# Self-attention scores of a one-layer graph network: the squares' off-diagonal block computed once and turned with the cross products, in one score buffer of two banks

## The reference

```
u     = x @ x.T / sqrt(384)                      # 256 x 256 scores, symmetric
p     = softmax(u);  delta = p * adj
attn  = delta / (sum(delta, axis=2) + 1e-10)
h_w   = x @ W_w.T + b_w                          # w in left, self, right
ctx   = (attn, j>i) @ h_left + diag(attn) * h_self + (attn, j<i) @ h_right
x     = layernorm(x + relu(layernorm(ctx) * gamma + beta))
```

## Time and profile before

| | |
|---|---|
| three runs | 472.43, 472.1, 472.37 us; median 472.37 |
| the profiled execution | 471.55 us, of which the span of the trace is 469.8 |
| TensorE busy | 456.4 us, 97% of the span |
| VectorE busy | 357.2 us, 76% |
| ScalarE busy | 325.3 us, 69% |
| GpSimd busy | 222.7 us, 47% |
| granted TensorE clock, mean | 0.996 of full speed |

### The profile page before, as it was taken

How to read it: one execution, slowest core, us unless ns; L and a number is a source line. 1 busy time by engine, 2 the same in 40 slices (tenths; PEclk the granted TensorE clock), 3 DMA queues, 4 the chain that set the end, 5 groups by cost and what they waited for, 6 DMA issues and landing times.

```text
span 469.8 us, 9613 instructions
## 1 busy us (share of the span) xinstructions
PE 456.4 (97%) x2714; PEld 452.4 (96%) x2714; DVE 357.2 (76%) x1087; ACT 325.3 (69%) x714; POOL 222.7 (47%) x294
## 2 busy tenths in 40 slices
PE   8999899999999999999999999999999999999992
PEld 6999899999999999999999999999999999999981
DVE  5777877777788777888777887777778877787766
ACT  7663787676687677677667678767668767767752
POOL 0115556544445543445554445654444554444552
PEclk9999999999999999999999999999999999999998
DMA  8476455566365566445566545555545556644211
GB/s 260 144 226 201 136 185 184 193 192 192 112 205 186 179 191 201 153 160 185 172 204 197 162 160 174 185 190 190 186 141 176 185 182 190 203 142 136 82 67 67
DMA packets 84582, 80.72 MB, mean 172 GB/s; under 512 B 7122, under 2 KB 76756, under 8 KB 84564
## 3 DMA queue, kind: packets, MB, share of 16 engines
q1 hardware_dynamic: 84560, 80.51, 53.6%
q10 hardware_dynamic: 4, 0.00, 0.0%
HBM read 51.91 MB, written 28.57 MB: 171 GB/s over the span
## 4 chain that ended last, share of the span: by engine, by line
PE 90%; POOL 3%; DVE 3%; issue 1%; ACT 1%; POOLq 0%; DVEq 0%
PE ps_proj L449 59%; PE ps_ctx L484 20%; PE ps_scores L441 4%; PE ps_scores L432 4%; PE ps_scores L395 1%; POOL shifted L1017 1%; POOL scaled L1013 1%; POOL rstd L1007 1%; PE ps_ctx L402 1%; DVE stats L774 1%; ACT normed L593 0%; PE ps_proj L490 0%; DVE xt_lo L706 0%; POOL dt_left L1001 0%; POOL dt_right L1001 0%
## 5 line engine op out<-in xcount | busy, mean ns | idle before, releaser
L449 PE MATMUL ps_proj<-w_hi,xt_hi 128*128 128x384 f32 x576 | 193.9, 337 | 2.1 <-ACT ps_proj L563 2.1
L449 PE MATMUL ps_proj<-w_lo,xt_hi 128*128 128x384 f32 x576 | 193.7, 336 | 0.0
L449 PE MATMUL ps_proj<-w_hi,xt_lo 128*128 128x384 f32 x576 | 193.6, 336 | 0.0
L1007 POOL TENSOR_TENSOR rstd<-var_eps,minus_half 128x4 f32<-128x4 f32 x32 | 43.8, 1368 | 182.7 <-DVE var_eps L793 180.2
L449 PEld LDWEIGHTS ps_proj<-w_hi,xt_hi 128*128 128x128 f32 x576 | 108.5, 188 | 2.7 <-ACT ps_proj L563 2.7
L449 PEld LDWEIGHTS ps_proj<-w_lo,xt_hi 128*128 128x128 f32 x576 | 108.3, 188 | 0.0
L449 PEld LDWEIGHTS ps_proj<-w_hi,xt_lo 128*128 128x128 f32 x576 | 108.2, 188 | 0.0
L567 ACT ACTIVATE proj_hi<-ps_proj 128x384 fp32r<-128x384 f32 x128 | 63.4, 496 | 55.5 <-PE ps_proj L449 55.0
L563 ACT ACTIVATE ps_proj<-bias 128x384 f32<-128x384 f32 (+1 forms) x192 | 92.9, 496 | 4.2 <-DVE proj_lo L759 3.9
L1013 POOL TENSOR_TENSOR scaled<-normed,gamma_sb 128x384 f32<-128x384 f32 x62 | 63.1, 1018 | 36.6 <-ACT normed L593 30.5
L759 DVE TENSOR_TENSOR proj_lo<-ps_proj,proj_hi 128x384 fp32r<-128x384 f32 x128 | 68.1, 547 | 13.5 <-ACT proj_hi L567 13.5
(11 more groups left out here) (86 smaller groups left out, 663.6 us busy)
## 6 DMA issues: line engine op xcount, KB each, us to landing
x_sb<-in_x SPq DMA_DIRECT2D x32, 384.0 KB, 4.4
xt_sb<-in_x_t SPq DMA_DIRECT2D x31, 384.0 KB, 3.8
out_dram<-out_sb SPq DMA_DIRECT2D x31, 384.0 KB, 2.9
adj_sb<-in_adj SPq DMA_DIRECT2D x32, 256.0 KB, 4.5
dt_dram<-turned SPq DMA_DIRECT2D x31, 256.0 KB, 2.0
dt_raw<-dt_dram SPq DMA_DIRECT2D x124, 64.0 KB, 2.0
cross_dram<-cross_turned SPq DMA_DIRECT2D x30, 256.0 KB, 2.1
cross_raw<-cross_dram SPq DMA_DIRECT2D x120, 64.0 KB, 2.0
```

The lines of the kernel that those rows point to most:

```text
L449: mm = nc.tensor.matmul(ps_proj[bank(at, g)][:, 0:H], stationary, moving[w][:, c, :], start=False, stop=True, skip_group_check=True)
L1007: nc.gpsimd.tensor_tensor(rstd[at.slot(2)][:], var_eps[:], minus_half[:], ALU.pow).then_inc(rstd_ready, 1)
```

## The change

The high and low parts of `x_t` now stand side by side in one tile, `xt_split`, so that one matmul can take keys of both. `squares` is gone. `cross(ahead)` does nine matmuls: for the first row tile, hi by hi of all 256 keys and hi by lo of all 256 keys; for the second row tile one matmul for each chunk with 384 columns (hi by hi of its own tile, hi by lo of both tiles). A row of `ps_scores` now has three blocks of 32 columns in each of the four groups (squares of the own tile, and two for what becomes the scores), in a bank of its own for each row tile. There is one such buffer instead of two. `turn_cross` transposes the last two blocks, so the squares' off-diagonal block, computed only in the first row tile, reaches the second one by the transpose.

`finish_scores` no longer waits for TensorE in these batches, but first adds the squares of the own tile onto `cross_raw` (a new instruction, with the semaphore `own_added`). `cross(ahead)` waits for the deltas of `ahead - 1`, which is `nxt`; before it was `ahead - 2`. Three batches instead of two are done in full; the third, batch 2, stands in batch 1 behind the first projection. On ScalarE `seed_proj(at, 4)` stands ahead of `exps(nxt)` in all batches; before it was so in batch 1 alone.

```diff
-    IN_FULL = 2
+    IN_FULL = 3
...
-        xt_hi = [sb(f"xt_hi{i}", [P, C, L], F32R) for i in range(UNROLL)]
-        xt_lo = [sb(f"xt_lo{i}", [P, C, L], F32R) for i in range(UNROLL)]
+        xt_split = [sb(f"xt_split{i}", [P, C, 2 * L], F32R) for i in range(UNROLL)]
...
-        ps_scores = [psum(f"ps_scores{i}", [P, T, L]) for i in range(2)]
+        ps_scores = psum("ps_scores", [P, T, BANK])
...
+        def blocks(t):
+            return ps_scores[:, t, 0:3 * P].rearrange("p (q k c) -> p q k c", q=Q, k=3)
+
+        def exponentials(t):
+            return ps_scores[:, t, 0:3 * P].rearrange("p (q e) -> p q e", q=Q)[:, :, R:3 * R]
...
                 if at.b == 0:
                     sp.dma_start(adj_sb[2][:], adj_rows[2]).then_inc(adj_loaded[2], 16)
-                    store_cross(ahead)
                     sp.dma_start(x_sb[0][:], x_rows[0]).then_inc(x_loaded[0], 16)
                     store_turned(nxt)
-                    load_cross(ahead)
                     load_turned(nxt)
...
             def scores_in_full(at):
+                if at.b != 0:
+                    pe.wait_ge(delta_ready, at.n(T, 0))
...
-                            mm = nc.tensor.matmul(ps_scores[at.slot(2)][:, t, :], stationary, moving, start=(c == 0 and t == 0 and i == 0),
+                            mm = nc.tensor.matmul(blocks(t)[:, :, 1:3, :], stationary, moving, start=(c == 0 and i == 0),
...
             def cross(at):
                 pe.wait_ge(xt_lo_ready, at.n(1, C))
-                pe.wait_ge(delta_ready, at.n(T, -T))
-                for t in range(T):
-                    for c in range(C):
-                        mm = nc.tensor.matmul(ps_scores[at.slot(2)][:, t, :], xt(at, c, t * P, (t + 1) * P)[0], keys(xt(at, c, 0, L)[1]),
-                                              start=(t == 0 and c == 0), stop=(c == C - 1), skip_group_check=True)
+                pe.wait_ge(delta_ready, at.n(T, 0))
+                tile = xt_split[at.slot(UNROLL)]
+                for c in range(C):
+                    nc.tensor.matmul(blocks(0)[:, :, 0::2, :], tile[:, c, 0:P], keys(tile[:, c, 0:L]),
+                                     start=(c == 0), stop=False, skip_group_check=True)
+                    nc.tensor.matmul(blocks(0)[:, :, 1:3, :], tile[:, c, 0:P], keys(tile[:, c, L:2 * L]),
+                                     start=False, stop=(c == C - 1), skip_group_check=True)
+                for c in range(C):
+                    mm = nc.tensor.matmul(blocks(1), tile[:, c, P:L], keys(tile[:, c, P:2 * L], 3),
+                                          start=(c == 0), stop=(c == C - 1), skip_group_check=True)
                 mm.then_inc(cross_ready, 1)
-            def squares(at):
-                pe.wait_ge(cross_turned_ready, at.n(1, 1 - IN_FULL))
...
-                    cross(ahead)
                     attend(at, 0)
                     attend(at, 1)
                     return
-                if nxt.exists(BATCHES):
-                    squares(nxt)
                 for i, g in enumerate(order(at)):
                     project(at, g)
+                    if at.b == 1 and g == 0:
+                        scores_in_full(nxt)
...
                 split_proj(at, 1)
-                if at.b == 1:
-                    seed_proj(at, 4)
+                seed_proj(at, 4)
                 if nxt.exists(BATCHES):
                     exps(nxt)
-                if at.b != 1:
-                    seed_proj(at, 4)
...
             def finish_scores(at):
-                if not in_full:
+                if in_full:
+                    dve.wait_ge(scores_ready, at.n(1, 1))
+                    nc.vector.memset(gate[:], 0.0)
+                else:
                     dve.wait_ge(cross_loaded, at.n(64, 64 * (1 - IN_FULL)))
-                dve.wait_ge(scores_ready, at.n(1, 1))
-                nc.vector.memset(gate[:], 0.0)
+                    own = cross_raw[:].rearrange("p a h (t r) -> p a (h t) r", t=T)[:, :, 0::T + 1, :].rearrange("p a t r -> p t a r")
+                    square = ps_scores[:, :, 0:3 * P].rearrange("p t (q k c) -> p t q k c", q=Q, k=3)[:, :, :, 0, :]
+                    nc.vector.tensor_tensor(own, own, square, ALU.add).then_inc(own_added, 1)
+                    dve.wait_ge(own_added, at.n(1, 1 - IN_FULL))
+                    nc.vector.memset(gate[:], 0.0)
...
-            turn_cross(first.plus(2))
             deltas(first.plus(1))
```

More of the change, by code:

```diff
@@ L210, in gnn_resnorm @@
         cross_ready = sem("cross_ready")
+        own_added = sem("own_added")
         cross_turned_ready = sem("cross_turned_ready")
@@ L419, in open_context, with keys @@
                     nc.tensor.matmul(ps_ctx[:, t, 0:HE], zeros[:, 0:P], zeros[:], start=True, stop=True).then_inc(ctx_opened, 1)
-            def keys(tile):
-                return tile.rearrange("p (h q c) -> p q h c", q=Q, c=R)
+            def keys(tile, n=T):
+                return tile.rearrange("p (h q c) -> p q h c", q=Q, h=n)
             def cross(at):
                 pe.wait_ge(xt_lo_ready, at.n(1, C))
-                pe.wait_ge(delta_ready, at.n(T, -T))
-                for t in range(T):
-                    for c in range(C):
-                        mm = nc.tensor.matmul(ps_scores[at.slot(2)][:, t, :], xt(at, c, t * P, (t + 1) * P)[0], keys(xt(at, c, 0, L)[1]),
-                                              start=(t == 0 and c == 0), stop=(c == C - 1), skip_group_check=True)
-                mm.then_inc(cross_ready, 1)
-            def squares(at):
-                pe.wait_ge(cross_turned_ready, at.n(1, 1 - IN_FULL))
-                for t in range(T):
-                    for c in range(C):
-                        mm = nc.tensor.matmul(ps_scores[at.slot(2)][:, t, :], xt(at, c, t * P, (t + 1) * P)[0], keys(xt(at, c, 0, L)[0]),
-                                              start=False, stop=(c == C - 1), skip_group_check=True)
-                mm.then_inc(scores_ready, 1)
+                pe.wait_ge(delta_ready, at.n(T, 0))
+                tile = xt_split[at.slot(UNROLL)]
+                for c in range(C):
[6 more added lines that the diff above has]
+                                          start=(c == 0), stop=(c == C - 1), skip_group_check=True)
+                mm.then_inc(cross_ready, 1)
             def product(at, g, c):
@@ L543, in exps @@
                 for t in range(T):
-                    nc.scalar.activation(ps_scores[at.slot(2)][:, t, :], ps_scores[at.slot(2)][:, t, :], ACT.Exp,
+                    nc.scalar.activation(exponentials(t), exponentials(t), ACT.Exp,
                                          bias=neg_max[:, t:t + 1], scale=-1.0,
@@ L705, in split_xt @@
                 dve.wait_ge(xt_hi_ready, at.n(1, C))
-                nc.vector.tensor_tensor(xt_lo[at.slot(UNROLL)][:], xt_sb[at.slot(UNROLL)][:],
-                                        xt_hi[at.slot(UNROLL)][:].bitcast(F32), ALU.subtract).then_inc(xt_lo_ready, 1)
+                tile = xt_split[at.slot(UNROLL)]
+                nc.vector.tensor_tensor(tile[:, :, L:2 * L], xt_sb[at.slot(UNROLL)][:], tile[:, :, 0:L].bitcast(F32),
+                                        ALU.subtract).then_inc(xt_lo_ready, 1)
             def turn_cross(at):
```

17 lines of the change are left out of this document (8 added, 9 removed).

## The result

The changed kernel takes 466.13 us (median of 4 runs, 465.89 to 466.30) against 472.40 for the kernel before (4 runs, 472.10 to 472.78): ratio 0.987, 95% interval 0.9858 to 0.9882. That is 6.3 us less; 466.0 was forecast. The profiled execution took 466.12 us with a span of 464.4 us, against 471.55 and 469.8 before, so the two spans, in which the parts can be read, differ by 5.4.

What follows compares the result with a forecast made beforehand. TensorE's matmuls were taken to bound the kernel. Steady batches 5.4, start 0.6 and end 0.55, less 0.2 for late loads, gain 6.35 us: 466.0 us from the 472.37 median, range 464.4 to 470.4.

Steps and rivals of the forecast that it cites:

- The steady batch: TensorE's score matmuls in steady batches fall from 1.43 to 1.23 us: 0.20 saved a batch, 27 x 0.20 = 5.4.
- late loads: Loads landing late in rare batches: 0.2 us in all taken off the gain.
- rival (b): Matmuls writing columns with gaps cost 0.174 instead of 0.118 us, giving about 477.8 us; chance 0.08.
- The cushion at cross: Cross now waits for the next batch's deltas, but is free 0.9 us before TensorE comes.
- What is late next: After the deltas: first residual meets GpSimd's beta (1.4 us), store_cross goes 0.95 later, split_delta waits 1.1 past the attend.
- moving seed_proj(4) costs nothing: On ScalarE in steady batches, the seed ahead of the exponentials keeps its lead: done at 201.1, needed at 202.15.
- rival (a): Loop over the dt loads, 13.5 us against a 13.76 batch, becomes the bound: 471.2, half way 468.5; chance 0.16.
- The start: Batches 0 to 2: earlier seed gains 1.2, longer cross gives back 0.52, deltas 0.1; batch 3 starts 0.6 earlier.
- The end: Batch 30 drops squares(31), 0.72 us; with a later load for batch 31's split_delta, 0.55 of it arrives.
- The sum: Steady batches 5.4, start 0.6, end 0.55, less 0.2 for late loads: 6.35 us gained.

Runs made afterwards that it cites:

- experiment 3: Changed kernel with VectorE's turn_cross ahead of residual(0): 466.20 us, ratio 0.9884.
- experiment 5: Changed kernel with each 384-column matmul of the second row tile split into two of 256 columns: 473.27 us, ratio 1.003.
- experiment 6: Changed kernel with each 384-column matmul of the second row tile split into one of 128 and one of 256 columns: 470.77 us, ratio 0.9971.
- experiment 1: Kernel before with only ScalarE's seed_proj(4) moved ahead of the exponentials in every batch: 471.40 us, ratio 0.999.
- experiment 2: Changed kernel with seed_proj(4) put back behind the exponentials except in batch 1: 474.68 us, ratio 1.0057.
- experiment 4: Changed kernel with two batches' scores in full instead of three: 470.19 us, ratio 0.9965.
- experiment 12: Kernel before, unchanged, once more under the profile: 471.68 us, span 470.0.
- 11: Changed kernel with turn_cross ahead of residual(0) and, in batch 2 alone, project(4)'s seed ahead of the normalisation, project(0)'s split ahead of the shift: 465.85 us.

## Why the forecast was right, and where its parts were not

The gain comes, as forecast, from the matmul time that fell away in the 27 steady batches (3 to 29), while everything else stayed under the new batch length. The single parts follow; that their sum met the measured time to 0.1 us is luck, as the last of them shows.

**The steady batch: right.** 0.187 us a batch instead of 0.20, 5.05 instead of 5.4 in all, and nothing off for late loads, in which experiment 3 finds no cost. Writes into columns with gaps cost nothing: 0.12 a matmul of 256 columns, so rival (b) is out. Splitting the wide matmuls (experiment 5) takes the gain back, and some 0.06 us a batch more. Its price was argued from columns plus a fixed part; experiment 6 shows more: a matmul of 128 columns costs nearly as much as one of 256. The gain is there because 384 is above that floor. The Trainium skill (TensorE: Matmul & The Clock Gate, "LDWEIGHTS (loading the stationary operand)") gives 128 weight columns over 1.2 GHz for a weight load, 0.107 us; the measured floor of 0.112 us, and the 0.11 to 0.12 between weight loads, agree with it. The Trainium skill (TensorE: Matmul & The Clock Gate, "Back-to-back issue gap") also gives 81 ns a matmul for a stream of 128-column matmuls. No run here has such a stream; taken for the 128 columns of a pair, it would make an estimated 0.20 us a pair, and 0.23 was measured.

**The cushion at cross: right, in size too, but not constant.** 0.9 was forecast; over the 27 steady batches it is 0.63 to 1.29 us, and with the loads on time (experiment 3) 0.84 to 0.89. The sum put the longer work behind a shift that stays. In 20 batches the shift's root was shorter, for a reason that I had not seen: the load of dt is now late in every batch (ScalarE starts on it 0.6 to 1.7 us after the attend), so VectorE's half of the split (L780) starts 0.05 us or more behind GpSimd's root, and the root takes 1.01 us instead of 1.40. In the 7 batches in which it starts up to 0.13 ahead, the root takes 1.43 to 1.54. Where the load is very late (1.3 us and more) the shift waits for the split instead, and that takes half or all of the gain back. So the late load, costed as a risk, gave 0.3 to 0.4 us in about half of the batches; in the others the shift came between 0.2 earlier and 0.2 later than before.

**What is late next: right in kind.** Residual 1.28 (forecast 1.4); split_delta waits for DMA, 1.06 us past the attend in the batch shown (195.68 against 194.62; forecast 1.1; 0.58 to 1.74 over the 27). SP's store_cross comes 0.5 later in the batch in half of them and up to 1.2 in the others (forecast 0.95). By the forecast's own sum ScalarE, with the seed ahead, is the last before the deltas and the own add is hidden beside it; experiment 1 bears this out, as the seed's move alone makes the residual long and the loads late. What the forecast then did not draw is that "moving seed_proj(4) costs nothing" already contains all of this lateness.

**The seed: the step with the wrong weight.** "Moving seed_proj(4) costs nothing" is right, 471.4 in experiment 1. The text priced what the move costs and not what it prevents. It named the two times, done at 201.1 and needed at 202.15, and did not ask for the first with the exponentials ahead: they start with the row maxima at 200.82, 0.9 for them and 0.5 for the seed give 202.2, which is about 0.1 late. Experiment 2 shows 0.25 a batch (the matmul starts 0.15 us behind the end of the seed, 204.56) and 8.5 us in all, more than the whole gain.

**The loop, rival (a): not the bound.** Forecast 13.5, measured 13.34 in the one batch of experiment 4 where it ran freely, against a batch of 13.77. It is near: in the last batches of the changed kernel, where a load lands up to 2.4 us after its issue, the chain goes through it at 13.67 (from 416.29 to 429.96, the landings of two loads). It takes over once VectorE has between 1.0 us (three adds, where it holds TensorE four times) and 1.65 us (five) more.

**The start: wrong by 1.0 us in the profiled pair, a third of it by the sum.** Forecast 0.6 gained, read 0.42 lost. The chain ahead of batch 2 is TensorE's from 5.91 us on, and its first 54 matmuls (scores and first 36 of the projections) took 10.52 us against 9.84, since the matmuls followed each other more slowly (every 0.21 us for 256 columns, 0.118 later) for longer. That is about half the speed, as the lower of the two clock levels would give, but the profile's granted clock is 1.00 there in both kernels (6 to 16 us), so that it is the clock is not shown. These 0.68 us are not the change's in full: the kernel before needed 10.32 in experiment 12. With them taken off batch 3 starts 0.26 earlier, and 0.16 earlier against experiment 12. So by a like start the forecast's 0.6 was 0.2 to 0.3. The seed gave what was forecast, 1.1 of 1.2 (project(4) at 48.79 - 0.68 = 48.11; 48.16 in experiment 1). What was given back was 0.8 and not 0.6: besides the 0.52 of the longer cross product, the first one waits for its deltas after all, 0.06 us in the chain, and its first matmul then takes 0.36 instead of 0.12, as project(4) after its own wait takes 1.83 instead of 1.56 (it did so before too).

**The end:** 0.79 instead of 0.55. All 0.72 of the squares of batch 31 arrive, though the last load is later: it lands 13.96 us after the attend of batch 29, 13.69 before. The deltas behind that attend end only 0.1 later instead of 0.4, and the root takes 1.01 us instead of 1.40, so the shift can wait for the late split and still be 0.07 early. The chain through the loads costs nothing that can be read: from the attend of batch 2 to the end it is 410.7 us here, and 410.6 and 410.7 in experiments 3 and 11, whose chains stay with TensorE up to 425.

**The sum** was 6.35 in spans; measured 5.4 in the profiled pair and 5.6 against experiment 12's span. The medians differ by 6.3. That the forecast of 466.0 was hit to 0.1 us is luck on top of a right mechanism: its gain was about 0.9 us too large in spans, from the start (0.3 by the sum, 0.7 by the slower first matmuls) and the steady batches (0.35) less the end and the late loads (0.4), and this fell in with a profiled execution of before that lay 0.85 us under its median, where the changed kernel's lay on its own.

## What to carry to other kernels

When a block of matmuls moves away from between two waits, list every small instruction that had been hidden under it, and compute where it stands without the reordering that comes with the change: here one 0.5 us seed decided between 1.3% faster and 0.6% slower. A matmul of 128 columns, each with its own weight load, cost nearly as much here as one of 256; joining the 128-column piece to the 256-column one saves. A row that says "busy" can hold a wait: compare the same group of matmuls (45 projections, 7.80 against 8.06) or the busy time of the weight loads between kernels before believing that TensorE waits for nothing.

## What the runs showed of the hardware

- A matmul of 128 columns with its own weight load took nearly as long as one of 256: pairs of 128 + 256 followed each other every 0.23 us (experiment 6), 384 columns every 0.174 to 0.177, 256 every 0.118. Matmuls that write columns with gaps (runs of 32 or 64) took the same 0.118.
- GpSimd's root on 4 elements a partition takes 1.39 to 1.54 us when VectorE's add of two tiles of SBUF (0.69) starts up to 0.17 us ahead of it, and then ends 1.56 us after the add's start; it takes 1.01 to 1.03 when the add starts 0.05 us or more behind it or runs elsewhere, and the add takes 0.69 either way. This holds for each root of the traces of the changed kernel and the one before.
- VectorE's residual beside GpSimd's beta takes 1.28 instead of 0.54 to 0.58 when beta starts 0.15 us ahead. Here whichever starts first makes the other longer: in experiment 2 the residual came first (206.62), took 0.54, and beta took 1.38.
- How long the matmuls run at half speed at the start differs between executions, though TensorE had done the same until 5.91 us in all of them. The first 54 matmuls took 9.84, 9.91 and 10.32 us in the three profiles with the old score buffer and 10.22 to 11.29 in the eleven with the new one. Three against eleven overlap, so whether the kernel's form has a part in it stays open; it would be worth up to 0.6 us.
